# Output projections of two batches in one step of a gated cross-attention, the first half of the heads weighed with high and low halves, and VectorE's order changed

## The chip, the cores and the metric

The kernel runs on one core of one Trainium2 chip, as one program in which SyncE issues the DMAs and TensorE, VectorE, ScalarE and GpSimd each run their own written-out order of instructions, tied by semaphores. The metric is the device time of one execution in microseconds; a version's number is the median of its runs. Before the change it is 667.44 us (3 runs, 667.02 to 667.79).

## The reference

The input `x` is 32 batches of 128 tokens by 128 features. A first layer adds gated cross-attention to a context of 128 tokens by 64 features per batch, with 16 heads of 64; a second adds a gated mixture of 32 experts (8 picked per token) and a shared one. All of it is float32.

```
attn(q, kv): scores = (q Wq)(kv Wk)^T / 8 per head;  softmax over the context;
             out = softmax (kv Wv);  return out Wo + bo
x = x + tanh(g_xattn) * attn(layernorm(x), ctx)
x = x + tanh(g_ffn)   * experts(layernorm(x))
```

The change lies in the first line of the two, the attention.

## The kernel before, in words

**Folding.** Wq and Wk are folded into one matrix a head, and Wv and Wo into `c_pair`, so that a batch needs: the projection `g` of its normed tokens with the folded matrix (L1161, one call for two batches), for each head a product of `g` with the context (the scores, transposed: context on the partitions), exp, a product of the exponents with the context itself (`weigh`, L1219), a division by the sum of the exponents (`normalise`, L802), and eight products with `c_pair` (`project_out`, L1245).

**Precision.** Most products are made of a high and a low half of each operand in the type fp32r, three products for one (L1148 to L1153, and L1207 to L1213 for the scores). `weigh`, `project_out` and the transposes are plain float32 products; the profile shows two matrix instructions for each of those.

**Batches and halves.** The batches go in chunks of four (`CB`), `t` is the batch and `b` its place in the chunk. Chunk 0 and chunk 7 are written out, chunks 1 to 6 are a hardware loop (L238). The heads of a batch come in two halves `h` (L232), each in two quarters `q`, which stand on different partitions (L235). PSUM has eight banks: two for the maxima's scores, two for the transposed scores, two for the weighed sums (`u_ps`), one for transposes and one small one.

**TensorE in batch t** (L1287): score products for the maxima of batch t+2, half 0 (L1176); transposed scores of t, half 0 (L1199); transpose of the maxima of t+1 (L1193); `weigh` of t-1, half 1, both quarters; in b = 1 the transpose of the next chunk's norm; `project_out` of t-3; maxima's products of t+2, half 1; scores of t, half 1; `weigh` of t, half 0, quarter 0; in odd batches `g_project` for two batches to come, which waits for VectorE to have taken the second-half maxima out of its banks; `weigh` of t, half 0, quarter 1.

**ScalarE in batch t** (L605): exp of half 0 into `probs_t` (L597); the transposed maxima out (L540); the weighed sums of t-1, half 1, out of PSUM (`u_out`, L545); in b = 1 the high half of the transposed norm (L526); exp of half 1; `u_out` of t, half 0, with the high half of `g` between its quarters in odd batches (L532).

**The sums' way.** Column 64 of the context operand is ones, so a row of the weighed sums is the sum of the exponents. SyncE spreads it by a DMA from row to partitions (`spread_sums`, L297), VectorE inverts it (L796), SyncE stores it to DRAM (L304) and reads it back broadcast over the partitions, in two DMAs, one a quarter (`spread_inverse`, L310); both wait until both quarters of the batch before have been normalised. `normalise` (L802) multiplies one quarter, 64 partitions by 1024, and waits for both DMAs.

**VectorE in batch t** (L997): maxima of t+2, half 0, both quarters (`take_max`, L788); statistics of batch t-4 after its residual (L707); `normalise` of t-2, quarter 0; in b = 1 the low half of the norm (L776); maxima of t+2, half 1; inversion of the sums of t-1; `normalise` of t-2, quarter 1; in odd batches the low half of `g` (`g_low`, L780), for which the score products of the next batch wait; the residual of t-3 (L811); the aggregate of the statistics (L712); in b = 3 a copy of the means (L717); in b = 0 the norm of the next chunk (`ln_apply`, L764).

**GpSimd in batch t** (L497): both halves of a piece of the experts' weights (L468), the gated bias (L479), both halves of the context of batch t+4 (L457), which wait for its DMA.

## Time and profile before

| | |
|---|---|
| median of 3 runs | 667.44 us (667.02 to 667.79) |
| the profiled execution, its own time | 668.55 us |
| its span, first to last instruction | 666.8 us |
| TensorE busy | 650.9 us, 98% of the span |
| VectorE busy | 498.9 us, 75% |
| ScalarE busy | 365.3 us, 55% |
| GpSimd busy | 284.6 us, 43% |
| mean granted TensorE clock | 0.999 of full speed |
| first score product of chunk 1 to that of chunk 7 | 60.87 to 316.34 us |

The ends of matrix instructions are modelled and they overlap one another by a little, so the busy time of TensorE is an upper measure; the distance between the starts of two instructions says what the first one occupied. The same holds in a smaller way for VectorE and ScalarE, where an instruction may start some 0.1 us before the recorded end of the one before. "Idle before" is the time in which an engine stood still in front of an instruction, with what released it. An engine that isn't the bound pays nothing for its idle time.

### The profile page before, as it was taken

How to read it: one execution, taken by the hardware profiler on the slowest of the kernel's cores; microseconds unless marked ns; L12 is line 12 of the kernel's file. 1: busy time of each engine (PE TensorE's matmuls, PEld its weight loads, DVE VectorE, ACT ScalarE, POOL GpSimd, SP SyncE). 2: the span in 40 equal slices, each digit the busy share in tenths (PEclk: the TensorE clock that was granted, in tenths of full speed). 3: DMA queues.
4: the chain of work that ended last, by engine and by line, in shares of the span. 5: the costliest groups of instructions: out<-in, count | busy, mean ns of one | idle time of the engine just before them, and what ended most of it. 6: DMA issues, size and time to landing. Idle time of an engine off the chain costs nothing.

```text
span 666.8 us, 13629 instructions
## 1 busy us (share of the span) xinstructions
PE 650.9 (98%) x3668; PEld 473.2 (71%) x3668; DVE 498.9 (75%) x1331; ACT 365.3 (55%) x690; POOL 284.6 (43%) x316
## 2 busy tenths in 40 slices
PE   8999999999999999999999999999999999999997
PEld 6656656667666666666657778788887878888785
DVE  6989858677586776776787968969596877869565
ACT  3564555465455555555465455555655655555553
POOL 4222323133132322234212655656565666657553
PEclk9999999999999999999999999999999999999999
DMA  8323322232323323233224825273654527374550
GB/s 188 94 64 82 92 63 70 63 91 63 80 62 79 94 62 79 62 79 83 63 67 130 192 62 134 83 170 99 141 133 98 134 72 164 81 162 112 131 142 16
DMA packets 63276, 65.58 MB, mean 98 GB/s; under 512 B 26112, under 2 KB 41600, under 8 KB 63232
## 3 DMA queue, kind: packets, MB, share of 16 engines
q1 hardware_dynamic: 63232, 65.07, 40.0%
q8 instruction: 18, 0.29, 0.2%
q14 instruction: 26, 0.21, 0.1%
HBM read 61.64 MB, written 2.88 MB: 97 GB/s over the span
## 4 chain that ended last, share of the span: by engine, by line
PE 68%; issue 8%; DMA 6%; DVE 6%; SPq 5%; POOL 4%; ACT 2%; DVEq 0%; POOLq 0%; ACTq 0%
PE bank L1151 13%; PE bank L1152 13%; PE bank L1153 13%; PE bank L1227 9%; PE bank L1251 5%; POOL halves L516 4%; PE bank L1187 3%; DMA inverse_bc<-inverse_dram 3%; PE bank L1207 2%; SPq L294 2%; DMA sums<-area 2%; DVE halves L783 2%; PE bank L1216 2%; PE bank L1213 2%; PE bank L1210 2%
## 5 line engine op out<-in xcount | busy, mean ns | idle before, releaser
L516 POOL TENSOR_TENSOR halves<-area,halves 128x512 fp32r<-128x512 f32 x134 | 173.9, 1298 | 141.3 <-ACT halves L650 137.8
L663 ACT ACTIVATE area<-bank 128x512 f32<-128x512 f32 x136 | 81.4, 599 | 116.1 <-PE bank L1153 115.1
L602 ACT ACTIVATE area<-bank 128x512 f32<-128x512 f32 x128 | 69.5, 595 | 118.7 <-PE bank L1216 118.7
L1107 DVE TENSOR_TENSOR bank<-area,bank 128x512 f32<-128x512 f32 x128 | 88.6, 692 | 53.4 <-PE bank L1153 53.2
L1227 PE MATMUL bank<-area,ctx_keys 128*65 128x512 f32 (+1 forms) x256 | 124.7, 600 | 0.5 <-ACT u_odd L550 0.4
L1151 PE MATMUL bank<-x2t_hi,w_hi 128*128 128x512 f32 x272 | 110.2, 405 | 0.1
L1152 PE MATMUL bank<-x2t_hi,w_lo 128*128 128x512 f32 x272 | 107.2, 394 | 0.0
L1153 PE MATMUL bank<-x2t_lo,w_hi 128*128 128x512 f32 x272 | 106.3, 391 | 0.0
L462 POOL TENSOR_TENSOR ctx_hi<-ctx_raw,ones_col 128x128 fp32r<-128x128 f32 x32 | 19.7, 615 | 200.4 <-DMA ctx_raw<-ctx_t 200.4
L792 DVE TENSOR_REDUCE row_max<-bank 128x4 f32<-128x512 f32 x128 | 81.7, 680 | 27.2 <-PE bank L1187 22.9
L650 ACT ACTIVATE halves<-area 128x512 fp32r<-128x512 f32 x136 | 85.0, 625 | 14.1 <-DVE area L1118 13.6
L1118 DVE TENSOR_TENSOR area<-bank,wbc 128x512 f32<-128x512 f32 x128 | 86.3, 679 | 0.0
L806 DVE TENSOR_TENSOR area<-u_odd,inverse_bc 64x1024 f32<-64x1024 f32 x32 | 40.6, 1269 | 45.1 <-DMA inverse_bc<-inverse_dram 44.6
L1251 PEld LDWEIGHTS bank<-c_pair,area 128*128 128x128 f32 x512 | 61.3, 192 | 12.6 <-issue 10.1
L1227 PEld LDWEIGHTS bank<-area,ctx_keys 128*65 128x65 f32 (+1 forms) x256 | 37.2, 164 | 39.6 <-issue 38.7
L1251 PE MATMUL bank<-c_pair,area 128*128 128x128 f32 x512 | 62.6, 276 | 1.2 <-DVE area L806 1.2
L1151 PEld LDWEIGHTS bank<-x2t_hi,w_hi 128*128 128x128 f32 x272 | 51.2, 188 | 12.1 <-DVE area L1118 1.8
L1153 PEld LDWEIGHTS bank<-x2t_lo,w_hi 128*128 128x128 f32 x272 | 51.2, 188 | 11.9
L1152 PEld LDWEIGHTS bank<-x2t_hi,w_lo 128*128 128x128 f32 x272 | 51.2, 188 | 10.3
L1187 PEld LDWEIGHTS bank<-ctx_hi,halves 64*128 64x128 f32 x512 | 33.5, 187 | 30.2 <-issue 22.3
L1151 PE MATMUL bank<-halves,w_hi 128*128 128x512 f32 x136 | 54.4, 400 | 0.5 <-POOL halves L516 0.5
L1153 PE MATMUL bank<-halves,w_hi 128*128 128x512 f32 x136 | 53.9, 396 | 0.0
(129 smaller groups left out, 1088.1 us busy)
## 6 DMA issues: line engine op xcount, KB each, us to landing
wbc<-rows_dram SPq DMA_DIRECT2D x126, 256.0 KB, 4.4
inverse_bc<-inverse_dram SPq DMA_DIRECT2D x64, 256.0 KB, 3.9
w_raw<-experts SPq DMA_DIRECT2D x32, 102.0 KB, 2.0
ctx_raw<-ctx_t SPq DMA_DIRECT2D x32, 64.0 KB, 1.8
ctx_keys<-ctx_nat SPq DMA_DIRECT2D x32, 64.0 KB, 2.1
out<-area SPq DMA_DIRECT2D x7, 256.0 KB, 3.9
max_rows<-max_t SPq DMA_DIRECT2D x64, 4.0 KB
area<-wq_t SPq DMA_DIRECT2D x1, 512.0 KB, 4.6
```

The source lines that it names most:

```text
L516: nc.gpsimd.tensor_tensor(hid_lo[:, u % SLOTS, :], hid[:, u % HIDS, :], raw(hid_hi[:, u % SLOTS, :]), ALU.subtract).then_inc(hidlo_ready, 1)
L602: nc.scalar.activation(probs_t[:, k, :, :], st_ps[q][:].rearrange("p (h n) -> p h n", h=4), ACT.Exp)\
L650: nc.scalar.activation(hid_hi[:, u % SLOTS, :], hid[:, u % HIDS, :], ACT.Copy).then_inc(hidhi_ready, 1)
L663: nc.scalar.activation(silu_g[:, u % 2, :], gate_ps[u % 2][:], ACT.Silu).then_inc(silu_ready, 1)
L792: nc.vector.tensor_reduce(row_max[:, parity, first:first + 4], ps[q][:].rearrange("p (h m) -> p h m", h=4), AX_X, ALU.max)\
L1107: nc.vector.tensor_tensor(up_ps[u % UPS][:], silu_g[:, u % 2, :], up_ps[u % UPS][:], ALU.mult)\
L1118: nc.vector.tensor_tensor(hid[:, u % HIDS, :], up_ps[u % UPS][:], wbc[:, group % WBC_SLOTS, i, :], ALU.mult).then_inc(hid_ready, 1)
L1151: nc.tensor.matmul(ps, wh, xh, start=start, stop=False)
L1152: nc.tensor.matmul(ps, wl, xh, start=False, stop=False)
L1153: return nc.tensor.matmul(ps, wh, xl, start=False, stop=stop)
L1227: nc.tensor.matmul(u_ps[q][0:CD + 1 if q == 0 else P, :], keys, probs_t[:, k, :, :].rearrange("p i n -> p (i n)"), start=True, stop=True). ...
L1251: ins = nc.tensor.matmul(ps, u_t[:, parity, p, :], c_pair[:, p, :], start=p == 0, stop=p == PAIRS - 1)
```

## The change

- **Weighing of half 0 in halves, chunks 1 to 6.** GpSimd splits the context operand of the batch (128x192) into `keys_hi` and `keys_lo` (`split_keys`), ScalarE copies the exponents of half 0 to `p_hi` (`probs_high`, two instructions of 128x512), VectorE subtracts them to `p_lo` (`probs_low`, two of 128x512), and TensorE makes three fp32r products a quarter in place of one float32 product (`weigh_halves`). Half 1 and chunks 0 and 7 stay as they are. The new tiles lie in memory that the expert stage uses later.
- **Output projections in pairs.** In an even batch of chunks 1 to 7 TensorE makes `project_out` of t-4 and t-3, one after the other, into two neighbouring pieces of the small bank; odd batches make none, but for batch 28 in the last. The projection of batch 0, before in chunk 0, is now in chunk 1. VectorE adds both at once (`residual_pair`, 128x256) and takes the statistics of two batches together in odd batches (`pair_stats`).
- **VectorE's order** in chunks 1 to 6 is written anew (`steady_attention`): in even batches the subtractions, the inversion and the first `normalise` stand ahead of the second-half maxima; in odd ones the statistics, the subtractions and the first `normalise` stand ahead of them, and inversion, `g_low` and the second `normalise` behind.
- **The inverse by quarters.** Each of the two DMAs of `spread_inverse` waits for its own quarter of `normalise` alone, and each `normalise` for its own DMA.
- ScalarE: `probs_high` behind the second-half `u_out` in even batches, ahead of it (with `xt_high` behind it in b = 1) in odd ones.

```diff
-NORM_AT = {(9, 1): ((NB - 1, 0),), (10, 1): ((NB - 1, 1),)}
+NORM_AT = {(8, 1): ((NB - 1, 0),), (9, 1): ((NB - 1, 1),)}
...
                 wait_first(inverse_out, 16 * t + 16)
                 for q in range(2):
                     wait_first(norm_ready[q], t)
-                for q in range(2):
                     sp.dma_start(inverse_bc[rows(q), :, :]...,
-                                 ...).then_inc(inverse_in, 16)
+                                 ...).then_inc(inverse_in[q], 16)
...
+            def split_keys(b, t, c):
+                pool.wait_ge(keys_in[b], 16 * c + 16)
+                wait(pool, u_done, 4 * (t - 2) + 4)
+                nc.gpsimd.tensor_tensor(keys_hi[:, b % 2, :], ctx_keys[:, b, :], ones_col[:].broadcast_to([P, 3 * CD]),
+                                        ALU.mult).then_inc(keyshi_ready, 1)
+                pool.wait_ge(keyshi_ready, t + 1 - HALVED_FROM)
+                nc.gpsimd.tensor_tensor(keys_lo[:, b % 2, :], ctx_keys[:, b, :], raw(keys_hi[:, b % 2, :]), ALU.subtract)\
+                    .then_inc(keyslo_ready, 1)
...
             def attention(c, first, last):
                 for b in range(CB):
                     t = CB * c + b
+                    if not first and not last:
+                        split_keys(b, t, c)
                     split_weights(b % 2, t, 2 * c + b // 2, NB if last else t + CB)
...
+            def probs_high(t):
+                act.wait_ge(exp_ready, 4 * t + 2)
+                wait(act, u_done, 4 * t - 2)
+                for q in range(2):
+                    nc.scalar.activation(p_hi[q], probs_t[:, q, :, :].rearrange("p h n -> p (h n)"), ACT.Copy)\
+                        .then_inc(phi_ready, 1)
...
+                    if not first and not last and b % 2 == 1:
+                        probs_high(t)
+                        if b == 1:
+                            xt_high(c + 1)
                     if not (first and b == 0):
                         for q in range(2):
                             u_out(t - 1, (b - 1) % 2, 1, q)
+                    if not first and not last and b % 2 == 0:
+                        probs_high(t)
...
+            def probs_low(t):
+                for q in range(2):
+                    dve.wait_ge(phi_ready, 2 * (t - HALVED_FROM) + q + 1)
+                    wait(dve, u_done, 4 * (t - 1) + q + 1)
+                    nc.vector.tensor_tensor(p_lo[q], probs_t[:, q, :, :].rearrange("p h n -> p (h n)"),
+                                            raw(p_hi[q]), ALU.subtract).then_inc(plo_ready, 1)
...
+            def residual_pair(t):
+                dve.wait_ge(bias_added, t + 2)
+                dve.wait_ge(attn_done, t + 2)
+                tiles = x_sb[:, bass.ds(t, 2), :].rearrange("p a d -> p (a d)")
+                nc.vector.tensor_tensor(tiles, small_ps[:, D:3 * D], tiles, ALU.add).then_inc(x2_ready, 2)
+
+            def pair_stats(t, b):
+                for i in range(2):
+                    batch_stats(t + i, b + i)
+                for i in range(2):
+                    batch_mean(t + i, b + i)
...
+            def steady_attention(c):
+                for b in range(CB):
+                    t = CB * c + b
+                    for q in range(2):
+                        take_max(t + 2, b % 2, 0, q)
+                    if b % 2 == 0:
+                        if b == 0:
+                            ln_apply(c + 1, t + CB)
+                        probs_low(t)
+                        invert(t - 1, 1)
+                        normalise(t - 2, 0, 0)
+                        for q in range(2):
+                            take_max(t + 2, 0, 1, q)
+                        residual_pair(t - 4)
+                        normalise(t - 2, 0, 1)
+                    else:
+                        pair_stats(t - 5, b - 1)
+                        if b == CB - 1:
+                            keep_means(t - b - CB)
+                        probs_low(t)
+                        normalise(t - 2, 1, 0)
+                        if b == 1:
+                            xt_low(c + 1)
+                        for q in range(2):
+                            take_max(t + 2, 1, 1, q)
+                        invert(t - 1, 0)
+                        g_low(2 * c + 2 + b // 2, b // 2)
+                        normalise(t - 2, 1, 1)
...
+            def weigh_halves(t, b, q):
+                if q == 0:
+                    pe.wait_ge(keyslo_ready, t + 1 - HALVED_FROM)
+                pe.wait_ge(phi_ready, 2 * (t - HALVED_FROM) + q + 1)
+                wait(pe, u_ready, 4 * (t - 1) + q + 3)
+                ...
+                nc.tensor.matmul(ps, keys_hi[:, b % 2, cols], p_hi[q], start=True, stop=False)
+                nc.tensor.matmul(ps, keys_lo[:, b % 2, cols], p_hi[q], start=False, stop=False)
+                pe.wait_ge(plo_ready, 2 * (t - HALVED_FROM) + q + 1)
+                nc.tensor.matmul(ps, keys_hi[:, b % 2, cols], p_lo[q], start=False, stop=True).then_inc(u_done, 1)
...
-                    if not (first and b < 3):
-                        project_out(t - 3, (b + 1) % 2, t + 1 if last and b == CB - 1 else t + 2)
+                    if b % 2 == 0 and not first:
+                        for i in range(2):
+                            project_out(t - 4 + i, i, t + 2, small_ps[:, (1 + i) * D:(2 + i) * D])
+                    if last and b == CB - 1:
+                        project_out(t - 3, 0, t + 1)
```

## Rows read from the trace of the kernel before

**Rows 1.** Busy time by stretch (columns: PE, PEld, DVE, ACT, POOL, PEclk, DMA share, GB/s).
```profile
60.00:316.00 256.00, 251.14 (x1686) 166.21 (x1688) 182.62 (x337) 138.44 (x270) 74.61 (x123) 1.00 0.30 74
330.00:360.00 30.00, 29.53 (x166) 18.89 (x165) 23.99 (x88) 16.53 (x33) 3.57 (x4) 1.00 0.26 66
```

**Rows 2.** Waits, 60 to 320 us (us in total, times, longest us).
```profile
DVE area L806 <- DMA inverse_bc<-inverse_dram: 44.8, 18, 5.1
```

**Rows 3.** Timeline, TensorE: first and last of 13 even batches (start us, us).
```profile
60.87 0.50 PE L1207 MATMUL bank<-halves,ctx_hi 64*128 64x512 f32 x2 [0.32 <-DVE halves L783]
...
316.34 0.50 PE L1207 MATMUL bank<-halves,ctx_hi 64*128 64x512 f32 x2
```

**Rows 4.** Timeline, TensorE, one pair of batches of chunk 3.
```profile
146.97 0.50 PE L1207 MATMUL bank<-halves,ctx_hi 64*128 64x512 f32 x2
...
149.92 1.95 PE L1251 MATMUL bank<-c_pair,area 128*128 128x128 f32 x16
151.80 0.66 PE L1187 MATMUL bank<-ctx_hi,halves 64*128 64x128 f32 x8
...
153.37 1.93 PE L1227 MATMUL bank<-area,ctx_keys 128*65 128x512 f32 x4
...
155.74 0.44 PE L1207 MATMUL bank<-halves,ctx_hi 64*128 64x512 f32 x2
...
162.52 1.07 PE L1227 MATMUL bank<-area,ctx_keys 128*65 128x512 f32 x2
163.54 0.39 PE L1151 MATMUL bank<-xnt_hi,a_hi 128*128 128x256 f32 x1
...
168.07 0.50 PE L1207 MATMUL bank<-halves,ctx_hi 64*128 64x512 f32 x2
```

**Rows 5.** Timeline, TensorE, expert stage: two products' first parts, three parts apart.
```profile
356.09 0.40 PE L1151 MATMUL bank<-x2t_hi,w_hi 128*128 128x512 f32 x1
...
356.78 0.40 PE L1151 MATMUL bank<-x2t_hi,w_hi 128*128 128x512 f32 x1
```

**Rows 6.** L1140 (duration ns min/median/max, first and last start us).
```profile
L1140 DVE TENSOR_TENSOR halves<-area,halves x2: 683/688/693, 660.0 to 660.6; 128x512 fp32r<-128x512 f32 x2
```

**Rows 7.** Timeline, the sums' way in an even batch.
```profile
151.30 1.18 SPq L302 DMA_DIRECT2D sums<-u_odd  x2
...
153.85 0.25 DVE L800 RECIPROCAL inverse<-sums 128x16 f32<-128x16 f32 x1
```

**Rows 8.** The chain of waits, a later batch's sums (start us, us, what).
```profile
181.66 1.87 DMA sums<-area
```

**Rows 9.** Timeline, VectorE, part of an odd batch.
```profile
225.21 1.22 DVE L806 TENSOR_TENSOR area<-u_odd,inverse_bc 64x1024 f32<-64x1024 f32 x1 [3.70 <-DMA inverse_bc<-inverse_dram]
226.35 1.28 DVE L792 TENSOR_REDUCE row_max<-bank 128x4 f32<-128x512 f32 x2
227.55 0.23 DVE L800 RECIPROCAL inverse<-sums 128x16 f32<-128x16 f32 x1
```

**Rows 10.** Timeline, VectorE, single instructions of chunk 2 and 3.
```profile
146.95 0.17 DVE L715 BATCH_NORM_AGGREGATE mean_var_now<-bn 128x2 f32<-128x6 f32 x1
147.36 0.17 DVE L720 COPY mean_var<-mean_var_now 128x8 f32 x1 [0.24 <-DVE mean_var_now L715]
...
149.22 0.28 DVE L710 BATCH_NORM_STATS2 bn<-x_sb 128x6 f32 x1
...
162.22 0.68 DVE L778 TENSOR_TENSOR xnt_lo<-bank,xnt_hi 128x512 fp32r<-128x512 f32 x1
162.82 1.27 DVE L792 TENSOR_REDUCE row_max<-bank 128x4 f32<-128x512 f32 x2
```

**Rows 11.** Timeline, VectorE and GpSimd side by side.
```profile
207.08 1.41 DVE L806 TENSOR_TENSOR area<-u_odd,inverse_bc 64x1024 f32<-64x1024 f32 x1
...
207.57 1.41 POOL L476 TENSOR_TENSOR w_lo<-w_raw,w_hi 128x204 f32 x1 [0.17 <-POOL w_hi L473]
```

**Rows 12.** Timeline, VectorE, last maxima of chunk 0.
```profile
54.10 1.29 DVE L792 TENSOR_REDUCE row_max<-bank 128x4 f32<-128x512 f32 x2
```

More of the change, by code:

```diff
@@ L154, in build @@
         x2t_lo = sb("x2t_lo", [P, 2, CT], F32R)
+        p_hi = [x[:, 1, :] for x in (x2t_hi, x2t_lo)]
+        p_lo = [x[:, 0, :] for x in (x2t_hi, x2t_lo)]
+        tail = slice(WCOLS - 2 * 3 * CD, WCOLS)
+        keys_hi, keys_lo = (w[:, tail].rearrange("p (s n) -> p s n", s=2) for w in (w_hi, w_lo))
         spare = sb("spare", [P, 2 * CB * NE])
@@ L615, in attention @@
                             u_out(t - 1, (b - 1) % 2, 1, q)
+                    if not first and not last and b % 2 == 0:
+                        probs_high(t)
                     if last and b == CB - 1:
                         x2t_out(1, scores_ps[1])
-                    if not last and b == 1:
-                        xt_high(c + 1)
+                    if first and b == 1:
+                        xt_high(1)
                     if last and b == 1:
@@ L1004, in attention @@
                                 take_max(t + 2, b % 2, h, q)
-                        if h == 0 and not first:
-                            batch_stats(t - CB, b)
                         if h == 1:
@@ L1019, in attention @@
                                 chunk_stats(n)
[L1020 removed]
+                        if h == 1 and b % 2 == 1 and first:
                             g_low(2 * c + 2 + b // 2, b // 2)
[L1022 to L1023 removed]
+                        if h == 1 and last:
+                            if b % 2 == 0:
+                                residual_pair(t - 4)
+                            if b == CB - 1:
                                 residual(t - 3)
[L1025 to L1028 removed]
+                            if b % 2 == 1:
+                                pair_stats(t - 5, b - 1)
+                            if b == CB - 1:
+                                keep_means(t - b - CB)
                         if first:
@@ L1031, in attention @@
                                 rstd_level(0, 1, slice(CB, 2 * CB), level)
-                        elif not last and step_of_chunk == 1:
-                            ln_apply(c + 1, t - b + CB)
                         if last:
@@ L1044, in attention @@
                             normalise(t - 2, b % 2, 0)
-                        if step_of_chunk == 2 and not last:
-                            xt_low(c + 1)
+                        if step_of_chunk == 2 and first:
+                            xt_low(1)
                         if step_of_chunk == 3 and last:
@@ L1191, in max_scores, with transpose_max @@
                             ins.then_inc(smax_done, 1)
-            def transpose_max(t, parity):
+            def transpose_max(t, parity, projected):
                 pe.wait_ge(max_ready, 4 * t + 4)
-                wait(pe, x2_ready, t - 4)
+                if projected is not None:
+                    wait(pe, x2_ready, projected)
                 wait(pe, maxt_ready, t)
@@ L1300, in attention @@
                     if not (last and b == CB - 1):
-                        transpose_max(t + 1, (b + 1) % 2)
+                        transpose_max(t + 1, (b + 1) % 2, t - 3 if b % 2 == 1 and not first else None)
                     if not started:
@@ L1315, in attention @@
                         pe.wait_ge(x2_ready, t - 3)
-                    if not (first and b < 3):
-                        project_out(t - 3, (b + 1) % 2, t + 1 if last and b == CB - 1 else t + 2)
+                    if b % 2 == 0 and not first:
[3 more added lines that the diff above has]
+                        project_out(t - 3, 0, t + 1)
                     if not (last and b >= 2):
@@ L1321, in attention @@
                     scores(t, b, 2 * c + b // 2, 1, 2 * c + b // 2 + 1, None)
-                    weigh(t, b, 0, 0, c + 1)
+                    if first or last:
+                        weigh(t, b, 0, 0, c + 1)
+                    else:
+                        weigh_halves(t, b, 0)
                     if last and b == 0:
@@ L1326, in attention @@
                         g_project(b // 2, c + 1, ((max_ready, 4 * (t + 2) + 3), (exp_ready, 4 * t + 3)))
-                    weigh(t, b, 0, 1, c + 1)
+                    if first or last:
+                        weigh(t, b, 0, 1, c + 1)
+                    else:
+                        weigh_halves(t, b, 1)
             pe.wait_ge(neg_ready, 2)
```

30 lines of the change are left out of this document (19 added, 11 removed).

## The prediction

> **What bounds the kernel now.** I read the busy table by stretch first. From 60 to 316 us, the six looped chunks of the attention (24 batches), TensorE is busy in 251.1 of 256 us, VectorE in 182.6, ScalarE in 138.4 and GpSimd in 74.6 [rows 1]. So TensorE sets the pace today, and VectorE has 29% of its time left. The waits then say how VectorE spends that time: 44.8 us of it go to 18 waits for the DMA that spreads the inverse sums [rows 2]. That is slack which a different order could use, and new work could fill it.
>
> The kernel repeats in pairs of batches, an even one and an odd one, since only odd batches hold the projection of the queries (`g_project`). As a mark of each batch I take **S**, the start of its first score product (L1207) on TensorE. The first S of the looped chunks is at 60.87 us and the S that follows the last pair is at 316.34 us, 12 pairs apart [rows 3]: 255.47/12 = **21.29 us a pair**. The pair from 146.97 to 168.07 [rows 4] shows where it goes. The even batch: 2.95 us to the output projection (scores, transpose, second-half weighing), 1.88 for one output projection (149.92 to 151.80), 1.57 for maxima and scores of the second half, then 2.37 from 153.37 to the next S at 155.74, of which two weighings and their gap take 1.87 and the maxima 0.50. Sum 8.77. The odd batch: 7.80 to the start of `g_project` (163.54), then 4.53 to the next S, which has to wait until VectorE has written the low halves of the projection.
>
> **The change on TensorE.** A weighing in float32 is replaced by three products of halves. In the expert stage three such products of 512 columns take 356.78 - 356.09 = 0.69 us [rows 5]. The two float32 weighings with the gap behind them took 1.87 [rows 4], so the saving is at most 1.87 - 1.38 = 0.49 us a batch. The new products have two more waits each, one of them between the second and the third product; no row prices them. Between zero saving and 0.49 I take 0.33, which leaves 0.16 of gap as it is. Over 24 batches that is 8 us. The pairing of the output projections saves no product: 1.88 us leaves the odd batch and enters the even one. So TensorE alone would need 8.77 + 1.88 - 0.33 = 10.3 us in an even batch, and in an odd one 7.80 - 1.88 - 0.17 = 5.75 to `g_project` (about 5.3 in the odd batch without the transpose of the norm: four products, an estimate of 0.47 from the sixteen matrix instructions in 1.88), then some 4.6: 20.2 to 20.7 a pair, 0.85 less than now.
>
> **ScalarE and GpSimd.** ScalarE gains two copies a batch. At some 0.6 us each (its mean instruction takes 138.4/270 = 0.51) that is 1.2 us a batch, and it is busy 138.4 of 256 us now [rows 1]: 29 us more still leave a third free. In even batches they stand behind the outputs of the second half and have the two projections as cover (3.8 us); in odd ones they delay those outputs by 1.2 us, which TensorE's next weighing just about meets. I cost both at nothing; without that cover the price is 0.4 us a pair. GpSimd gains two splits of 128x192 a batch, 1.1 us, and is busy 29% of the time: nothing by itself. SyncE issues the same DMAs. Its wait for the two halves of `normalise` is split, so the first half of the inverse leaves and lands a normalise earlier, and nothing behind it is late: its next load waits for a maximum 2.8 us after S anyway.
>
> **The change on VectorE, where I expect the time to be decided.** It gains two subtractions of 128x512 a batch; the nearest instructions, both inputs in SBUF and the same output type, start 0.62 us apart [rows 6], so 1.24 us a batch, 30 us over the loop. Busy time becomes 213 of 256: it still fits, but the order matters. In an even batch the inversion of the sums now stands ahead of the second-half maxima. It can't start before its DMA: today that issue begins at 151.30 [rows 7], and in a later batch the DMA landed 1.87 us after its second issue began [rows 8], so some 2.5 us after the first. The inversion starts at 153.85, 6.88 after S [rows 7], and nothing in the change makes the sums come earlier, since exponents, maxima and the second-half outputs in front of them stand as before. From there on everything on VectorE is in series up to the maximum that lets `g_project` start in the odd batch:
> - inversion 0.28; normalise 1.14 (225.21 to 226.35); two maxima 1.20 (226.35 to 227.55) [rows 9]; residual of two batches, 128x256, taken as 0.33 from the 0.28 of a 128x128 instruction [rows 10] and 128 more columns; second normalise 1.14;
> - in the odd batch two maxima 1.20; statistics of two batches: 0.28 each less the 0.08 by which a maximum's pair overlaps what follows (1.28 busy, the next 1.20 later) [rows 9, 10], then an aggregate that waits for the one before it, 0.41 as the aggregate and the copy behind it (146.95, 147.36) [rows 10], together 0.90; two subtractions 1.24; normalise 1.14; the low half of the norm 0.60 (162.22 to 162.82) [rows 10], in the first odd batch only; first maximum to `g_project` 0.72 (162.82 to 163.54) [rows 4, 10].
>
> That is 6.88 + 0.28 + 1.14 + 1.20 + 0.33 + 1.14 + 1.20 + 0.90 + 1.24 + 1.14 + 0.60 + 0.72 = 16.8 us from S to `g_project`, about 0.15 more where the subtraction waits for ScalarE's copy. In the other odd batch 0.60 goes and 0.45 comes (the copy of the means). TensorE could be there at 10.3 + 5.3 to 5.75 = 15.6 to 16.05; it would stand idle for 0.9 us before `g_project`. Then 4.6 to the next S: the low halves again close this stretch, so the cheaper weighing in it gives nothing back. A pair takes 21.25 to 21.55, in the mean 21.4, against 21.29 now. **The gain on TensorE is spent in a new wait for VectorE's maxima**, in place of the wait for the inverse.
>
> **Contention.** A normalise that ran beside a GpSimd subtraction took 1.41 us against 1.22, and the GpSimd instruction 1.41 as well, where GpSimd's 123 instructions take 74.6/123 = 0.61 in the mean [rows 1, 9, 11]. The change adds four GpSimd instructions a pair with SBUF inputs, and four VectorE subtractions with two of them, now all on the serial stretch. I take one more collision a pair at 0.2 us; the ends are 0 and, with a collision for each of the four, 0.8. The Trainium skill (SBUF — State Buffer, "SBUF: two separate sides") states it harder: a VectorE instruction with two SBUF inputs and a GpSimd one that reads SBUF exclude each other for a whole instruction. Here the trace agrees on GpSimd's side and shows only 0.2 us on VectorE's; the page's rule taken fully is a rival below.
>
> **The ends of the attention.** The projection of batch 0 leaves chunk 0, but there VectorE's maxima start at 54.10 with no idle time in front of them [rows 12]: they wait for VectorE's own earlier work and not for TensorE, so nothing is won. The last chunk gets five output projections in place of four, with TensorE busy in 29.53 of 30 us [rows 1]: +1.9 us; the ends are 0 and 1.9.
>
> **Sum.** 12 pairs times (21.4 + 0.2 - 21.29 = 0.3) = +3.6, plus 1.9 = +5.5 us. The profiled execution took 668.55 us, which makes 674; the median of the runs shown is 667.44, 1.1 lower, and on that scale it is **672.5 us**.
>
> **Rivals.**
> - *TensorE stays the bound (faster).* If VectorE's serial stretch is shorter by 0.9 us a pair than I add up, or the inversion starts sooner, the pair falls to TensorE's own 20.4: 12 x (-0.87) + 1.9 = -8.6 us, **659 us**. For it: VectorE's busy share would be only 83%, and the DMA waits of [rows 2] vanish. Against it: the start of the inversion is pinned at 6.88 by a DMA, and some fifteen instructions follow without a gap. It decides the sign from the point where the stretch from S to `g_project` falls under 16.5 us in the mean. 0.18 for the whole of it, 0.12 for a part (661 to 666).
> - *An even exchange.* No further collision, and the extra projection of the last chunk is hidden: 12 x 0.1 = +1.2, **668 us**. 0.13.
> - *GpSimd blocks VectorE for whole instructions (slower still).* By the rule each of the four new instructions, 0.6 us by that mean of 0.61, costs VectorE its full length where it meets one of the four normalises and four subtractions, some 7 of 21 us. With the subtractions' own share of the old GpSimd work that is about 0.8 us a pair: 12 x 0.9 + 1.9 = +12.7, **680 us**. 0.10.
>
> My forecast has 0.47. A measurement of this kernel can tell about 0.2% (1.3 us) from no change. So faster 0.30, same 0.13, slower 0.57. The range takes in the first rival at its lower end and stops short of the last: 659 to 679.
>
> **What would show it.** In the profile after: the products of L1151 in the attention should have idle time in front of them released by VectorE's maxima, near 0.9 us in each of 12 odd batches; the waits of normalise for the DMA should be almost gone; the inversion in even batches should start 6.9 us after S; the pair should be at 21.4 to 21.7 us. The weighings in halves should take 0.69 each. I am wrong if the pair is under 21, with TensorE's idle time before L1151 small, or if TensorE waits in front of the weighings for the high or low halves, which would be a chain I cost at nothing.

## The result and the profile after

The changed kernel takes **686.27 us** (686.17 to 686.52) beside 667.44 (667.02 to 667.79), five runs each: **1.0285** [1.0273, 1.0296]. It is slower by 18.8 us, where some 5 were forecast, and outside the range of 659 to 679. The sign was right, the size was not.

The busy lines of the page, and of the two stretches of [rows 1] (columns: us, then busy us and instructions by engine, the granted clock's share of full speed, DMA share, GB/s):

```profile
span 684.7 us, 13979 instructions
...
PE 653.0 (95%) x3716; PEld 477.0 (70%) x3716; DVE 537.8 (79%) x1365; ACT 385.0 (56%) x738; POOL 318.8 (47%) x364
```

```profile
60.00:316.00 256.00, 237.15 (x1625) 160.26 (x1626) 205.08 (x350) 148.47 (x300) 100.32 (x157) 0.99 0.26 70
330.00:360.00 30.00, 29.39 (x196) 19.43 (x194) 25.06 (x56) 14.72 (x32) 10.55 (x15) 1.00 0.27 69
```

TensorE has fallen from 251.1 to 237.15 busy of 256 us. No other engine is full: VectorE 205.08, ScalarE 148.47. So the kernel is held by an order of waiting, not by an engine's throughput. The granted clock stays at 0.99 of full speed, the 2.4 GHz level, and has no part in it: the five runs, at 0.996 to 1.000 in the mean, lie within 0.35 us of each other.

The first score products of the looped chunks and of the last chunk (L1293 now; compare [rows 3]):

```profile
61.12 0.50 PE L1293 MATMUL bank<-halves,ctx_hi 64*128 64x512 f32 x2 [0.32 <-DVE halves L817]
...
332.94 0.50 PE L1293 MATMUL bank<-halves,ctx_hi 64*128 64x512 f32 x2 [0.17 <-issue]
```

The loop takes 271.82 us, **22.65 a pair** against 21.29: 16.3 of the 17.9 us by which the span grew. Another 1.3 (351.76 from the second mark to the end of the span, against 350.46) lie behind it, where the last chunk has its fifth output projection. The rest, 0.25, lies ahead of the loop.

Waits from 60 to 330 us that bear on the change, out of a longer list (us in total, times, longest):

```profile
ACT u_odd L570 <- DVE area L848: 27.7, 16, 2.5
ACT area L570 <- DVE area L848: 22.1, 13, 2.4
PEld bank L1236 <- DVE row_max L826: 20.4, 12, 1.9
DVE inverse L842 <- DMA sums<-u_odd: 18.2, 12, 3.3
PE bank L1236 <- DVE row_max L826: 14.6, 11, 1.4
```

The wait for the inverse's DMA, 44.8 us [rows 2], has left the list, as forecast. TensorE's wait in front of `g_project` (L1236) for the maxima is there too. It was there before the change as well (L1151), but small on TensorE itself:

```profile
PE bank L1151 <- DVE row_max L792: 2.8, 6, 1.2
```

The first two rows were not forecast: **ScalarE stands some 50 us in `u_out` (L570) behind `normalise` (L848)**. This is one pair, VectorE and TensorE around the start of an even batch and ScalarE through it (start, duration, in brackets the idle time before and its releaser):

```profile
151.87 0.62 POOL L494 TENSOR_TENSOR w_lo<-w_raw,w_hi 128x204 f32 x1 [0.17 <-POOL w_hi L491]
151.90 1.67 DVE L848 TENSOR_TENSOR area<-u_odd,inverse_bc 64x1024 f32<-64x1024 f32 x1
152.01 0.50 PE L1293 MATMUL bank<-halves,ctx_hi 64*128 64x512 f32 x2 [0.20 <-DVE halves L817]
152.44 1.44 POOL L501 TENSOR_TENSOR x_sb<-x_sb,bo_gated 128x128 f32 x1
153.66 0.60 ACT L570 ACTIVATE u_odd<-bank 128x512 f32<-128x512 f32 x1 [2.51 <-DVE area L848]
154.17 1.08 ACT L622 ACTIVATE area<-bank 128x512 f32<-128x512 f32 x2
155.15 0.25 ACT L563 ACTIVATE max_t<-bank 16x128 fp32r<-16x128 f32 x1
155.54 3.81 PE L1350 MATMUL bank<-c_pair,area 128*128 128x128 f32 x32
155.65 1.43 SPq L303 DMA_DIRECT2D max_rows<-max_t  x2
157.19 1.18 SPq L311 DMA_DIRECT2D sums<-u_odd  x2
159.75 0.25 DVE L842 RECIPROCAL inverse<-sums 128x16 f32<-128x16 f32 x1 [1.45 <-DMA sums<-u_odd]
```

The new order has the second `normalise` as the last instruction of the batch. `u_out` waits for it, since it writes the buffer (`u_raw`, two by parity) that this `normalise` reads. ScalarE works in order, so the exponents of the next batch, whose scores are ready, stand behind that copy. They start at 154.17, 2.16 us after S, where they stood 1.31 after it before (148.28 in the pair of [rows 4]). The lateness of 0.85 is passed on: `max_out` (L563) copies the maxima behind the exponents, SyncE's two loads of the maxima (L303) wait for that copy, and the issue of the sums (157.19) stands behind these loads in SyncE's queue. So the inversion starts at 159.75, **S + 7.74** where the forecast had 6.88. Even the two output projections (L1350) start at S + 3.53 where they stood at 2.95. They wait for `max_out`, and the weighing ahead of them has itself waited for ScalarE's late copy.

### The profile page after: what moved, and what is told of

Read it like the earlier page. It is cut to its first block, busy times and chain, and to the rows that moved or that the text cites. A ratio compares the mean times of both kernels' runs of the same rounds, so it can differ in the third digit from the quotient of the medians.

```text
span 684.7 us, 13979 instructions
## 1 busy us (share of the span) xinstructions
PE 653.0 (95%) x3716; PEld 477.0 (70%) x3716; DVE 537.8 (79%) x1365; ACT 385.0 (56%) x738; POOL 318.8 (47%) x364
## 4 chain that ended last, share of the span: by engine, by line
PE 64%; DVE 11%; issue 10%; POOL 4%; ACT 3%; DMA 3%; SPq 3%; DVEq 1%; POOLq 0%; ACTq 0%
PE bank L1236 15%; PE bank L1238 14%; PE bank L1237 14%; PE bank L1326 5%; PE bank L1350 4%; POOL halves L536 4%; DVE row_max L826 3%; DVE area L848 3%; DMA sums<-u_odd 2%; PE bank L1272 2%; SPq L303 2%; PE bank L1293 2%; PE bank L1363 1%; ACT area L622 1%; DVE halves L817 1%
## 5 line engine op out<-in xcount | busy, mean ns | idle before, releaser
L1236 PE MATMUL bank<-x2t_hi,w_hi 128*128 128x512 f32 x272 | 110.3, 405 | 0.1
L470 POOL TENSOR_TENSOR ctx_hi<-ctx_raw,ones_col 128x128 fp32r<-128x128 f32 x32 | 14.6, 455 | 187.2 <-DMA ctx_raw<-ctx_t 109.9
L684 ACT ACTIVATE halves<-area 128x512 fp32r<-128x512 f32 x136 | 85.1, 626 | 17.2 <-DVE area L1203 16.9
L1326 PE MATMUL bank<-area,ctx_keys 128*65 128x512 f32 (+1 forms) x160 | 80.2, 612 | 0.5 <-ACT u_odd L570 0.2
L1350 PEld LDWEIGHTS bank<-c_pair,area 128*128 128x128 f32 x512 | 58.7, 192 | 12.8 <-issue 12.7
L1350 PE MATMUL bank<-c_pair,area 128*128 128x128 f32 x512 | 61.2, 277 | 0.9 <-ACT max_t L563 0.4
L1236 PEld LDWEIGHTS bank<-x2t_hi,w_hi 128*128 128x128 f32 x272 | 51.1, 188 | 12.5 <-DVE area L1203 2.1
L570 ACT ACTIVATE u_odd<-bank 65x512 f32<-65x512 f32 x64 | 36.3, 585 | 34.6 <-DVE area L848 33.3
L1236 PE MATMUL bank<-halves,w_hi 128*128 128x512 f32 x136 | 54.3, 399 | 0.5 <-POOL halves L536 0.5
L1237 PE MATMUL bank<-halves,w_lo 128*128 128x512 f32 x136 | 53.5, 393 | 0.0
```

What stands on the lines that cost most here:

```text
L684: nc.scalar.activation(hid_hi[:, u % SLOTS, :], hid[:, u % HIDS, :], ACT.Copy).then_inc(hidhi_ready, 1)
L1236: nc.tensor.matmul(ps, wh, xh, start=start, stop=False)
L1237: nc.tensor.matmul(ps, wl, xh, start=False, stop=False)
L1326: nc.tensor.matmul(u_ps[q][0:CD + 1 if q == 0 else P, :], keys, probs_t[:, k, :, :].rearrange("p i n -> p (i n)"), start=True, stop=True). ...
L1350: ins = nc.tensor.matmul(ps, u_t[:, parity, p, :], c_pair[:, p, :], start=p == 0, stop=p == PAIRS - 1)
```

## The experiments

The theory: the buffer of `u_raw` is what was missed. The second `normalise` at the end of a batch holds up ScalarE, and with it all that follows. The rivals blame the halves themselves (more instructions on VectorE and GpSimd, whatever the order), or the pairing and the order, whatever the halves. Each expectation says which theories it sets against each other. The short names e1 to e12 stand for the runs below. "Before" beside each result is the kernel before on the same chip.

**e1: one normalise earlier in odd batches.**

```diff
                         invert(t - 1, 0)
-                        g_low(2 * c + 2 + b // 2, b // 2)
                         normalise(t - 2, 1, 1)
+                        g_low(2 * c + 2 + b // 2, b // 2)
```

> The changed kernel with one line moved on VectorE: in odd batches of chunks 1 to 6 the second normalise stands ahead of g_low, as in the kernel before. Theory A (the profile after: ScalarE waits 56 us for normalise before it may empty the weighed sums into the buffer that normalise still reads, so the next exponents start 0.85 us late in even batches, and with them the sums, the inversion and all that follows): the exponents start 1.3 us after S again in even batches, the pair falls by 0.7 to 0.9 us, 8 to 11 us in all, about 677 us. Theory B (the recorded forecast's: only the length of VectorE's own series counts, and g_low's end releases the scores): normalise ahead of g_low puts 1.2 us in front of it, less the 0.8 us it idles there, so the pair grows by 0.3 to 0.5 us: about 690 us.

Measured: 678.69 us, 1.0189 [1.0170, 1.0209]; 22.17 a pair. Four instructions of VectorE swapped with one in every odd batch give back 7.3 us against the repeat of the changed kernel below (685.95), so the place of that `normalise` is worth over a third of the loss. In the pair from 151.31 the exponents start 1.31 after S and the inversion at S + 6.91 again. The rest of the loss is still there, and with it ScalarE's waits in the even batches, for the second `normalise` of these: 19.1 us in 13 waits.

**e2: the order and the pairing without the halves.** The looped batches weigh in float32; ScalarE's copies, GpSimd's splits and VectorE's subtractions for it go.

```diff
-                    if first or last:
-                        weigh(t, b, 0, 0, c + 1)
-                    else:
-                        weigh_halves(t, b, 0)
+                    weigh(t, b, 0, 0, c + 1)
```

> The changed kernel with the float32 weighing in all batches: no split of the keys, no high copies, no subtractions; pairs of projections, VectorE's order and the inverse by quarters stay. Theory A (the waits of ScalarE behind normalise, which the order makes, carry at least half of the loss; the work of the halves the rest): 2.5 us a pair leave VectorE, but normalise still ends behind g_low; 672 to 677 us. Theory B (the added work is the whole loss, the new order is harmless): 2.5 us of subtractions out of the series, TensorE is the bound again at 21.0 to 21.3 us a pair, 667 to 670 us, no slower than before.

Measured: 666.69 us, 1.0021 [1.0011, 1.0031]; 21.06 a pair, at or just under what theory B gave and well under theory A. ScalarE still waits for `normalise`, but VectorE has room for it:

```profile
DVE inverse L836 <- DMA sums<-u_odd: 49.6, 12, 4.8
ACT u_odd L568 <- DVE area L842: 26.2, 12, 2.3
```

ScalarE waits 43 us (26.2 and 17.2 in the row for the other buffer), and yet the whole kernel is only 0.2% behind the one before, since VectorE is idle 49.6 us in front of the inversion and can, as far as these lists tell, make up for it. A wait's length alone doesn't tell its price.

**e3: the halves in the old order, without the pairing.** This is the kernel before with the weighing in halves added; the cut shows where its subtractions stand.

```diff
                         if h == 0 and not first:
                             batch_stats(t - CB, b)
+                            if not last:
+                                probs_low(t)
```

> The kernel before with the weighing in halves alone (split keys, high copies, subtractions behind the first maxima and statistics); projections one a batch, VectorE's old order, both inverse DMAs behind both normalises. Theory A (the halves fit into VectorE's idle time where the order keeps normalise early; the loss is the order's): 664 to 670 us. Theory B (the work of the halves costs in any order, since the subtractions sit in front of the maxima that g_project waits for): 676 to 684 us.

Measured: 671.09 us, 1.0090 [1.0070, 1.0110]; 21.41 a pair, between the two theories. Even in the old order the busier VectorE makes ScalarE wait longer for `normalise`, 19.8 us where it was 5.5. So the parts alone cost 0.2% and 0.9%, and both together 2.85% (3.1% beside the kernel before on this chip): the loss is an **interaction**. The reading that fits the lists is that the halves take VectorE's slack, and the order makes ScalarE depend on how late VectorE is.

**e4: the keys split only once.** GpSimd's two splits a batch are left out in the loop, so later batches are weighed with stale keys.

```diff
             def attention(c, first, last):
                 for b in range(CB):
                     t = CB * c + b
-                    if not first and not last:
-                        split_keys(b, t, c)
```

> The changed kernel, but GpSimd splits the keys only twice, ahead of the attention, and not in each batch (the products of later batches use stale keys: that split is left out of the computation). Theory A (GpSimd's extra work costs only by single collisions of 0.2 to 0.4 us): 2 to 5 us less, 681 to 684 us. Theory B (GpSimd's instructions hold VectorE up for whole lengths, the reason of the miss): 10 us less or more, 676 us or under.

Measured: 679.92 us, 1.0212 [1.0195, 1.0229]; 22.15 a pair, between the two theories. GpSimd's splits, costed at nothing but a share of a collision, cost some 6 us in this kernel (685.95 less 679.92), while GpSimd is busy 39% of the loop. What they lengthen is `normalise` (60 to 330 us; the last numbers are busy us, mean ns of one; without the splits first, then the changed kernel):

```profile
L847 DVE TENSOR_TENSOR area<-area,inverse_bc 64x1024 f32<-64x1024 f32 x24 | 29.4, 1224 | 0.4
L847 DVE TENSOR_TENSOR area<-u_odd,inverse_bc 64x1024 f32<-64x1024 f32 x24 | 29.6, 1235 | 0.4
```

```profile
L848 DVE TENSOR_TENSOR area<-area,inverse_bc 64x1024 f32<-64x1024 f32 x24 | 32.6, 1360 | 0.4
L848 DVE TENSOR_TENSOR area<-u_odd,inverse_bc 64x1024 f32<-64x1024 f32 x23 | 30.9, 1345 | 0.3
```

Over 48 of them the difference of the means is 5.9 us, as much as the whole kernel gained. Not each of these lies on the chain that holds the kernel, so the agreement is no proof.

**e5: four buffers in place of two.** `u_raw` gets two more, in `wbc`, which the attention doesn't use. This takes away what makes ScalarE wait, with the order of VectorE as it is.

```diff
-        u_raw = (u_even, u_odd)
+        u_raw = (u_even, u_odd, wbc[:, 0:2], wbc[:, 2:4])
...
-                wait(act, norm_ready[q], t - 1)
+                wait(act, norm_ready[q], t - 3)
```

> The changed kernel with four buffers for the weighed sums in place of two (the two new ones lie in wbc, which the expert stage fills later), so ScalarE's copy of batch t waits for the normalise of t-4 and not of t-2; nothing else is moved. Theory A (that wait is the missing part of the loss): ScalarE's waits of 56 us for normalise go to zero, the exponents start 1.3 us after S in every batch, the inversion 6.9 us after S, and the pair falls from 22.65 to 21.6 to 21.9 us, near the recorded sum: 9 to 12 us less than the changed kernel, some 673 to 676 us. Theory B (the copies are late, but the series behind the maxima sets the pace whatever they do, as the run with normalise ahead of g_low, 22.17 a pair, might suggest): less than 5 us gained, 680 us or more.

Measured: 676.20 us, 1.0159 [1.0128, 1.0190]; **21.81 a pair**. The waits of `u_out` for `normalise` are gone, and the exponents start 1.30 after S again (theory A):

```profile
150.36 0.50 PE L1293 MATMUL bank<-halves,ctx_hi 64*128 64x512 f32 x2 [0.20 <-DVE halves L817]
...
151.66 1.08 ACT L622 ACTIVATE area<-bank 128x512 f32<-128x512 f32 x2 [1.46 <-PE bank L1302]
...
157.26 0.25 DVE L842 RECIPROCAL inverse<-sums 128x16 f32<-128x16 f32 x1 [1.19 <-DMA sums<-u_odd]
...
167.82 0.39 PE L1236 MATMUL bank<-xnt_hi,a_hi 128*128 128x256 f32 x1 [1.32 <-DVE row_max L826]
```

The inversion is at S + 6.90 and `g_project` at S + 17.46, against 7.74 and 18.34. The 0.88 less is nearly the 0.84 by which the mean pair fell (22.65 to 21.81). Of the pair, TensorE's 1.32 before `g_project` is left: the forecast's serial stretch on VectorE. The kernel is still 1.6% slower than the one before, so the sign of the forecast rests on that stretch and not on the missed wait. One pair of the twelve stands out, the one from 83.62 to 106.98, with 23.36 us: the sums' DMA landed late in it, and the inversion waited 2.92. The other eleven take 21.67 in the mean.

**e6 and e7: the two kernels again, on the same chip.** No edit to the kernel after, and none to the kernel before.

> The changed kernel as it is, on the chip of the others, for comparison: both theories expect 2.8 to 2.9% over the kernel before (684 to 687 us), with 22.65 us a pair.

> The kernel before as it is, for a trace of its pairs on this chip: the run with float32 weighing in the new order had 21.06 us a pair and yet was 0.2% slower in time than the kernel before there. If the pair of the kernel before is 21.1 or less here (theory A), its trace on record was of a slower execution and new order and pairing give the loop nothing; if it is 21.3 (theory B), they give 2.8 us in the loop and the last chunk takes more than that back.

Measured: 685.95 us, 1.0310 [1.0280, 1.0339], with 22.59 a pair; and 664.79 us in one run, with a loop of 20.97 a pair. The trace of before on which the forecast rests shows 21.29. The loop of before was thus 0.3 a pair longer in the trace on record than here, while the changed kernel's is the same within 0.06. The medians say the same: the kernel before is 2.0 us faster here (665.42), the changed one 0.3, so the ratio is 1.0310 here and 1.0285 there.

**e8: VectorE's order with both normalises early.** In even batches both stand ahead of the inversion; in odd ones the first stands behind the maxima of the second half. Two buffers, as in the changed kernel.

```diff
                         probs_low(t)
-                        invert(t - 1, 1)
                         normalise(t - 2, 0, 0)
+                        normalise(t - 2, 0, 1)
+                        invert(t - 1, 1)
                         for q in range(2):
                             take_max(t + 2, 0, 1, q)
                         residual_pair(t - 4)
-                        normalise(t - 2, 0, 1)
                     else:
...
                         probs_low(t)
-                        normalise(t - 2, 1, 0)
                         if b == 1:
                             xt_low(c + 1)
                         for q in range(2):
                             take_max(t + 2, 1, 1, q)
+                        normalise(t - 2, 1, 0)
                         invert(t - 1, 0)
```

> The changed kernel with VectorE's order of chunks 1 to 6 written once more: in even batches both normalises straight behind the subtractions, then inversion, maxima, residual; in odd ones the maxima straight behind the subtractions (and the low half of the norm), then first normalise, inversion, g_low, second normalise. Theory A (what costs is the maxima late for g_project and normalise late for ScalarE; the work of the halves itself fits): g_project has no idle time released by maxima, even batches 10.3 us, the pair 20.8 to 21.4: 662 to 670 us. Theory B (VectorE is simply full with the subtractions, in any order): the pair stays over 21.8, 675 us or more.

Measured: 671.62 us, 1.0095 [1.0066, 1.0125]; 21.40 a pair, the upper end of theory A. One normalise is now in the idle time ahead of the inversion, and TensorE's wait of some 14 us in front of `g_project` for the maxima has left its list. But ScalarE still stands behind the odd batches' normalises:

```profile
189.83 0.50 PE L1293 MATMUL bank<-halves,ctx_hi 64*128 64x512 f32 x2 [0.27 <-DVE halves L817]
191.24 0.60 ACT L570 ACTIVATE u_odd<-bank 128x512 f32<-128x512 f32 x1 [2.61 <-DVE area L848]
191.74 1.08 ACT L622 ACTIVATE area<-bank 128x512 f32<-128x512 f32 x2
```

**e9: that order with four buffers.** The edits of e5 and e8 together.

> Both remedies together: VectorE's order with early normalises and early maxima (as in the run before) and the four buffers for the weighed sums. Theory A (ScalarE's wait for the second normalise is what is left there: 1.2 to 2.6 us in front of its copies, late exponents and a late high half of the projection): even batches 10.2 us, odd ones 10.4, the pair 20.6 against 20.97 of the kernel before, with 1 us lost in the last chunk: 661 to 664 us, a little faster than the kernel before. Theory B (TensorE is by then held by GpSimd's context split and by VectorE's low half of the projection anyway): the pair 21.0 to 21.3, 666 to 670 us, no faster.

Measured: **659.94 us, 0.9908 [0.9893, 0.9924]**; 20.46 a pair, a little better than theory A. It beats both kernels. From 61 to 307 us:

```profile
61.00:307.00 246.00, 241.55 (x1730) 173.14 (x1732) 209.47 (x374) 161.61 (x318) 92.92 (x167) 1.00 0.29 76
```

TensorE is busy in 241.55 of 246 us: it is the bound again, and 20.46 is what the prediction's first rival gave (20.4).

**e10: four buffers and the keys split once.** The changed kernel's order; the edits of e4 and e5.

> The changed kernel with four buffers, and the keys split only twice ahead of the attention (that split is left out of the later batches). It asks how much of the 0.4 us a pair that GpSimd's splits cost in the changed kernel came through the late second normalise. Theory A (most of it: a collision lengthened the normalise that ScalarE waited for): under 0.2 us a pair is left, 674 to 676 us. Theory B (collisions lie on VectorE's own series too): 0.3 to 0.5 us a pair again, 671 to 673 us.

Measured: 672.78 us, 1.0110 [1.0089, 1.0130]; 21.54 a pair. With the buffers the splits cost 0.27 a pair (21.81 less 21.54), 3.2 us; the forecast had 0.2. With two buffers it was 0.44. The 0.27 is no typical pair: 1.96 of the 3.2 us lie in the pair of e5 in which the sums' DMA landed late, and the other eleven differ by 0.12.

**e11: four buffers without VectorE's subtractions.** The low halves of the exponents aren't computed; the third product takes the high half a second time.

```diff
-                        probs_low(t)
                         normalise(t - 2, b % 4, 0)
```

> The changed kernel with four buffers, without VectorE's two subtractions a batch; the third product takes the high half again, so TensorE's work is the same (the low half of the exponents is left out of the computation). Theory A (the recorded forecast: in the odd batch 1.24 us of subtractions stand on the series from the inversion to the maxima that g_project waits for, those of the even batch lie in front of the inversion and cost nothing): the pair falls by 1.1 to 1.25 us to 20.6 to 20.8, 660 to 663 us. Theory B (another wait, the inversion's or GpSimd's, takes over at once): 0.6 us a pair or less, 668 us or more.

Measured: 663.31 us, 0.9961 [0.9947, 0.9974]; 20.69 a pair. The subtractions cost 21.81 - 20.69 = 1.12 us a pair, a term that the forecast put at 1.24 in the odd batch's stretch (1.00 without the pair of e5 that stands out). VectorE now waits 57 us in front of the inversion for the sums.

**e12: the better version in float32.** e9 with the weighings as before and no halves.

> The fastest version so far (early normalises and maxima, four buffers for the weighed sums) with the float32 weighing in all batches. It asks what the weighing in halves is worth where nothing waits for VectorE. Theory A (TensorE sets the pace in both, and the halves save the difference of the products): the pair rises from 20.46 to 20.85 to 21.05 us, 5 to 7 us more, 665 to 667 us, the level of the kernel before. Theory B (the gain came from order and buffers alone, and the halves bring nothing): 660 us as well.

Measured: 663.48 us, 0.9971 [0.9961, 0.9982]; 20.76 a pair, between what the two theories gave. So of e9's gain of 0.92%, order, buffers and pairing bring 0.29% and the halves 0.63%: 0.30 us a pair, 0.15 a batch. The two traces show where. In an even batch the distance from the first weighing of half 0 to the maxima's products behind both, with halves and in float32:

```profile
152.14 0.45 PE L1313 MATMUL bank<-x2t_hi,w_hi 128*65 128x512 f32 x1
...
153.68 0.66 PE L1272 MATMUL bank<-ctx_hi,halves 64*128 64x128 f32 x8
```

```profile
152.35 1.93 PE L1318 MATMUL bank<-area,ctx_keys 128*65 128x512 f32 x4
154.21 0.66 PE L1264 MATMUL bank<-ctx_hi,halves 64*128 64x128 f32 x8
```

That is 1.54 against 1.86, **0.32 saved**, in ten of the twelve even batches (the first two lose about 0.3 each). In odd batches the distance from the first weighing to the next S is 5.34 against 5.43 in the mean: 0.1 saved, since that S waits for VectorE's low half of `g`, as the prediction said.

## Why the prediction was wrong

**The step that failed** is this one: "nothing in the change makes the sums come earlier, since exponents, maxima and the second-half outputs in front of them stand as before", by which the inversion was pinned at S + 6.88. Nothing made them earlier, but the moved `normalise` made them later: the exponents stand 0.85 us later, the inversion starts at S + 7.74, and the wait behind it costs 0.84 a pair (e5). It was followed to the one who reads its output (the DMA waits of SyncE, VectorE's own queue), and not to the one who waits to overwrite its input: `u_out`, and behind it in ScalarE's queue the exponents. The trace of before had the sign of it in its list of waits (L550 and L806 are `u_out` and `normalise` there):

```profile
ACT area L550 <- DVE area L806: 5.5, 13, 1.6
```

5.5 us in 13 waits then, nearly all in one buffer (the other had one wait of 0.5); 50 us in 29 waits now, in both.

Point by point, on the pair from 152.01:

- *Serial stretch from S to `g_project`*, 16.8 forecast. Measured S + 18.34: 0.86 of the difference of 1.5 is the late inversion, the rest lies on the way behind it. These are VectorE's rows:

```profile
159.75 0.25 DVE L842 RECIPROCAL inverse<-sums 128x16 f32<-128x16 f32 x1 [1.45 <-DMA sums<-u_odd]
159.95 1.22 DVE L848 TENSOR_TENSOR area<-area,inverse_bc 64x1024 f32<-64x1024 f32 x1
161.09 1.28 DVE L826 TENSOR_REDUCE row_max<-bank 128x4 f32<-128x512 f32 x2
162.29 0.41 DVE L865 TENSOR_TENSOR x_sb<-bank,x_sb 128x256 f32 x1
162.72 1.48 DVE L848 TENSOR_TENSOR area<-area,inverse_bc 64x1024 f32<-64x1024 f32 x1
164.23 1.29 DVE L826 TENSOR_REDUCE row_max<-bank 128x4 f32<-128x512 f32 x2
165.55 0.49 DVE L744 BATCH_NORM_STATS2 bn<-x_sb 128x6 f32 x2
165.99 0.51 DVE L749 BATCH_NORM_AGGREGATE mean_var_now<-bn 128x2 f32<-128x6 f32 x2
166.67 0.69 DVE L835 TENSOR_TENSOR x2t_hi<-area,x2t_hi 128x512 fp32r<-128x512 f32 x1 [0.17 <-ACT x2t_hi L630]
167.28 0.68 DVE L835 TENSOR_TENSOR x2t_lo<-area,x2t_lo 128x512 fp32r<-128x512 f32 x1
167.88 1.21 DVE L848 TENSOR_TENSOR area<-u_odd,inverse_bc 64x1024 f32<-64x1024 f32 x1
169.02 0.68 DVE L812 TENSOR_TENSOR xnt_lo<-bank,xnt_hi 128x512 fp32r<-128x512 f32 x1
169.62 1.27 DVE L826 TENSOR_REDUCE row_max<-bank 128x4 f32<-128x512 f32 x2
```

  From the inversion to `g_project` (170.35) it is 10.60, forecast 9.9. Of that 0.7 the second `normalise` is 0.37 (162.72 to the maximum at 164.23 is 1.51, where 1.14 was taken), the statistics 0.22 with the wait of 0.17 for ScalarE's copy, the two maxima ahead of them 0.12, the residual 0.10; the inversion gave 0.08 back. The 0.37 is a collision, which the forecast had as a term of its own. The list of instructions and their order was right.

- *`g_project` waits for the maxima*, 0.9 forecast in each of 12 odd batches: 14.6 us in 11 waits, 1.33 each, where it was 2.8 us in 6.
- *Collisions*, 0.2 a pair: 0.44 with two buffers, where they also lengthen the very `normalise` for which ScalarE waits (e4); 0.27 with four, or 0.12 without the pair that stands out (e10). The term was worked out from a `normalise` of 1.41 in [rows 11], and what stretched it was misread: see the last section.
- *The pair*, 21.6 with the collision: with four buffers 21.81, with two 22.65. The 0.84 between them is the missed wait, some 10 us of the 13.8 by which the median missed the forecast. With four buffers 2.5 us over the forecast are left in the loop, 1.7 of them in the one pair that stands out. Two smaller parts lie outside the loop: the prediction took 1.1 off for the profiled execution of before, and that of the changed kernel is only 0.2 above its median; and its own terms add up to 672.9, not 672.5 (668.55 + 5.5 - 1.1).
- *Saving on TensorE*, 0.33 a batch. The products are nearly as cheap as said, 0.75 where 0.69 was given: one weighing in halves takes 161.60 - 160.85:

```profile
160.85 0.45 PE L1313 MATMUL bank<-x2t_hi,w_hi 128*65 128x512 f32 x1
...
161.60 0.40 PE L1313 MATMUL bank<-x2t_lo,w_hi 128*128 128x512 f32 x1
```

  Where TensorE is the bound, the saving is the forecast one in even batches, 0.32, and 0.1 in odd ones, where the low halves of `g` close the stretch; with the first two even batches, which lose, that makes 0.15 a batch (e9 against e12).
- *The last chunk*, 1.9 for its extra projection: 1.3.
- *Rivals.* "TensorE stays the bound" comes about only with another order and the buffers: e9. "GpSimd blocks VectorE for whole instructions" forecast 680, nearest in number, and that is luck: its mechanism is at work (last section), but the splits cost 3 to 6 us (e4, e10), where the rival put the collisions at some 10, and it doesn't hold the missed wait. A meeting costs `normalise` the rest of GpSimd's instruction, 0.2 to 0.45 us, and not 0.6, and only 20 of 47 pay it.

Settled by removing it is the wait for the buffer. Of the remaining 0.2 a pair between e5 and the forecast, 0.14 come from the one pair with the late sums; why their DMA landed late there, in e4 too, no run shows. How the rest divides between collisions, maxima and statistics was read from one pair only.

## What to carry to other kernels

When an instruction moves later in its queue, ask not only who reads its result but **who waits to overwrite what it reads**, and what stands in that engine's queue behind the waiting instruction: here a copy that nobody was in a hurry for held up the exponents. Look up every such wait in the trace of before, even one of 1 us, and give it the new start time of its releaser. And test the parts alone and together: two edits of +0.2% and +0.9% made +2.85%, while the same halves with `normalise` moved early and two more buffers made -0.9%.

## What was not expected of the hardware

- **Of a `normalise` and a GpSimd instruction that meet, the one that starts first runs through, and the other stands.** In the trace the standing is no idle time; it is inside the duration of the instruction. The pair above shows both sides. GpSimd's L494 starts at 151.87, 0.03 ahead of the `normalise` at 151.90, and has 0.59 left to run; the `normalise` takes 1.67 where an undisturbed one takes 1.22. L501 starts at 152.44, inside that `normalise`, and takes 1.44 where it takes 0.46 alone; it ends at 153.88, 0.31 behind the end of the `normalise`.

  This holds over the loop. Of the 47 instances of `normalise` that the trace of the changed kernel lists singly, 20 take 1.40 to 1.67, and in each of the 20 a GpSimd instruction had started before it and was still running. In 14 a GpSimd instruction started only later, and all 14 take 1.22, as do the 13 that meet none. The kernel before shows the same: seven of 50 take 1.31 to 1.58, each with a GpSimd instruction ahead of it, and the 14 with only a later one take 1.22. One of the seven is the `normalise` of [rows 11], whose rows show the GpSimd instruction behind it; the one that stretched it by 0.19 had 0.33 left to run:

```profile
206.88 0.53 POOL L473 TENSOR_TENSOR w_hi<-w_raw,ones_col 128x204 f32 x1 [0.24 <-POOL ctx_lo L465]
```

  So the prediction took 0.2 as the price of meeting GpSimd, where it was the rest of one GpSimd instruction. The change adds two GpSimd instructions a batch and shifts the starts on both engines: 20 stretched ones in place of seven. GpSimd pays more: in its split of the weights the mean went from 701 ns to

```profile
L491 POOL TENSOR_TENSOR w_hi<-w_raw,ones_col 128x204 f32 x24 | 24.5, 1020 | 0.0
```

  The Trainium skill (SBUF — State Buffer, "SBUF: two separate sides") has whichever starts first hold a shared port for its whole instruction while the other stands; these rows agree, on VectorE's side and on GpSimd's.

- **The kernel before is not one number**: it took 667.44 us in the runs on record and 665.4 to 665.8 in those of the experiments, on three chips, and the loop of its two traces takes 21.29 and 20.97 a pair. A term of 0.1 us a pair (1.2 us in all) is smaller than that, and one trace beside another can't tell it.
